# Attention scores turned in 64-row pieces: even rows into one PSUM bank, odd rows into the other

## The reference, cut to what matters

```python
a = softmax(q @ k.T * scale)      # 64 x 64 for each batch and head
o = a @ v
```

## Time and profile before

| what | us |
|---|---|
| median of 3 runs | 2369.84 (2367.78 to 2382.06) |
| the profiled execution | 2368.65 |
| its span, first to last instruction | 2366.8 |
| TensorE matmul busy | 2017.6 (85%) |
| VectorE busy | 1704.2 (72%) |
| ScalarE busy | 1203.9 (51%) |
| GpSimd busy | 1166.3 (49%) |

### The profile page before, as it was taken

One profiled execution on the slowest core, in us unless ns is written; L12 is line 12 of the kernel. 1 busy time (PEld: TensorE's weight loads), 2 busy tenths in 40 slices (PEclk: granted clock), 3 DMA queues, 4 the chain that ended last, 5 costly groups with the idle time before them and its releaser, 6 DMA issues.

```text
span 2366.8 us, 64773 instructions
## 1 busy us (share of the span) xinstructions
PE 2017.6 (85%) x25996; PEld 1681.2 (71%) x25996; DVE 1704.2 (72%) x4619; ACT 1203.9 (51%) x2802; POOL 1166.3 (49%) x1408
## 2 busy tenths in 40 slices
PE   5999989899899998998989685994888897997981
PEld 3976768777687776876767464993677786886981
DVE  6688787887878878888778984224888888874232
ACT  5356775466744677446755342552433342443540
POOL 3674346752367533675245543445554513214476
PEclk7999999999999999999999896997998998998996
DMA  3000000000000000000000018992001000117993
GB/s 139 4 7 1 2 1 4 5 3 2 2 4 5 3 2 1 4 5 3 2 37 2 20 40 216 347 351 79 22 17 28 14 8 16 35 37 240 351 336 94
DMA packets 98044, 147.33 MB, mean 62 GB/s; under 512 B 32016, under 2 KB 72464, under 8 KB 97488
## 3 DMA queue, kind: packets, MB, share of 16 engines
q1 hardware_dynamic: 88656, 124.55, 15.6%
q0 software_dynamic: 9088, 18.63, 3.0%
HBM read 126.55 MB, written 16.58 MB: 60 GB/s over the span
## 4 chain that ended last, share of the span: by engine, by line
PE 52%; DVE 25%; POOL 10%; issue 7%; ACT 4%; DMA 2%; SPq 0%; POOLq 0%; DVEq 0%; ACTq 0%
PE PS L636 5%; PE PS L2016 5%; PE PS L2000 5%; PE PS L1519 4%; PE PS L1525 4%; POOL GOT L1667 3%; PE PS L1023 3%; PE PS L988 2%; DVE mx L1017 2%; PE PS L1088 2%; DVE P L1019 2%; PE PS L1038 2%; DVE zo L612 2%; PE PS L1087 2%; PE PS L1119 2%
## 5 line engine op out<-in xcount | busy, mean ns | idle before, releaser
L2029 ACT ACTIVATE wh<-PS,we 128x128 f32<-128x128 f32 x624 | 176.4, 372 | 203.6 <-PE PS L2000 202.9
L1913 POOL DMA_INDIRECT wx<-x,INV x156 | 149.2, 956 | 179.5 <-PE PS L2007 136.1
L1017 DVE TENSOR_REDUCE mx<-PS 128x8 f32<-128x512 f32 x256 | 176.6, 690 | 36.7 <-PE PS L999 24.7
L616 POOL TENSOR_TENSOR xrs<-xrs,Cs 128x2 f32<-128x2 f32 x112 | 80.4, 717 | 234.4 <-DVE xrs L608 232.6
L2016 PE MATMUL PS<-we,wh 128*128 128x128 f32 x1248 | 172.1, 280 | 22.0 <-DVE wxT L2046 20.9
L2000 PE MATMUL PS<-wxT,we 128*128 128x128 f32 x1248 | 169.7, 283 | 22.1 <-issue 11.4
L1019 DVE TENSOR_TENSOR P<-PS,mx 128x512 f32<-128x512 f32 x256 | 176.9, 691 | 8.9
L1540 ACT ACTIVATE eh<-PS 128x256 f32<-128x256 f32 x256 | 96.8, 384 | 160.2 <-PE PS L1519 155.9
L2016 PEld LDWEIGHTS PS<-we,wh 128*128 128x128 f32 x1248 | 155.7, 193 | 28.4 <-DVE wxT L2046 26.7
L1023 PE MATMUL PS<-Cs,P 128*128 128x128 f32 x1024 | 157.0, 284 | 22.1 <-ACT P L1413 12.9
L2000 PEld LDWEIGHTS PS<-wxT,we 128*128 128x128 f32 x1248 | 157.0, 199 | 24.0 <-issue 12.2
(11 more groups left out here) (349 smaller groups left out, 5613.4 us busy)
## 6 DMA issues: line engine op xcount, KB each, us to landing
we<-in_wf SPq DMA_DIRECT2D x78, 578.0 KB, 6.1
we<-in_wl SPq DMA_DIRECT2D x78, 578.0 KB, 6.5
yf<-wy SPq DMA_DIRECT2D x78, 64.0 KB, 5.7
ys<-wy SPq DMA_DIRECT2D x78, 64.0 KB, 6.4
x<-X SPq DMA_DIRECT2D x32, 128.0 KB, 2.1
R<-in_wa SPq DMA_DIRECT2D x1, 3072.0 KB, 14.9
wx<-x,INV POOLq DMA_INDIRECT x156, 5.8
X<-in_x SPq DMA_DIRECT2D x4, 512.0 KB, 15.0
```

Of the source, the lines that this page charges most:

```text
L1017: e.tensor_reduce(A.mx[r], S3, AX, ALU.max).then_inc(*o.inc())
L1913: e.indirect_dma_start(out=WB[s].x[n_ % 2], out_offset=None, in_=x1[half_of(q)], in_offset=bass.IndirectOffsetOnAxis(ap=INV[half_of(q)][:, ...
L2029: i = e.activation(B.h[:, 128 * f:128 * f + 128], ps(s, 1)[:, 128 * f:128 * f + 128], ACT.Relu, bias=w[:, 512 + f:513 + f])
```

## The change

`pe_turn_p` now handles both r of a unit in one step. It takes the 128 x 128 transposes apart: for each r and k, the upper 64 partitions (parity 0) of `P[r]` go as a 64 x 128 block into bank 0, and the lower 64 (parity 1) as another into bank 1. A unit has 16 transposes of 64 moving columns in place of 8 of 128. The step waits for both exponentials (or masks) and raises one semaphore. ScalarE's two copies go bank by bank as before, but a bank now holds one parity of both r; they have one wait in front of them. `pe_heads` waits for both copies in either call, and finds its operand at another place of the same size. `STEPS` has one `a_pT` in the place of two, and the strings of `ORDER` for all engines and both lists are written anew (in the first sweep's list, TensorE has 64 steps less, and in the rest 64 less).

```diff
-        def pe_turn_p(e, dst, P):
-            for k in range(4):
-                i = e.transpose(dst[:, 128 * k:128 * k + 128], P[:, 128 * k:128 * k + 128], ID)
+        def pe_turn_p(e, s, P):
+            for r, k, p in product(range(2), range(4), range(2)):
+                a, c0 = slice(64 * p, 64 * p + 64), 64 * (4 * r + k)
+                i = e.transpose(ps(s, p)[:, c0:c0 + 64], P[r][a, 128 * k:128 * k + 128], ID[a, a])
             return i
...
             for q, i, p in product(range(2), range(2), range(2)):
-                c0, q0 = 66 * (2 * q + i), W * q + 128 * i + 64 * p
-                j = e.matmul(dst[64 * p:64 * p + 64, c0:c0 + 66], A.P[r][:, q0:q0 + 64],
+                c0, q0 = 66 * (2 * q + i), 256 * r + 64 * (2 * q + i)
+                j = e.matmul(dst[64 * p:64 * p + 64, c0:c0 + 66], A.P[p][:, q0:q0 + 64],
...
                 for r in range(2):
                     e.wait_ge(*(sig.at(G, "a_ex", a, u, r) if a else sig.at(G, "a_mk", u, r)))
-                    pe_turn_p(e, ps(s, r), A.P[r]).then_inc(*sig.inc(G, "a_pT", a, u, r))
-                    yield
+                pe_turn_p(e, s, A.P).then_inc(*sig.inc(G, "a_pT", a, u))
+                yield
                 for r in range(2):
-                    e.wait_ge(*sig.at(G, "a_pt", a, u, r))
+                    e.wait_ge(*sig.at(G, "a_pt", a, u, 1))
                     pe_heads(e, A, ps(s, r), r, u).then_inc(*sig.inc(G, "a_ops", a, u, r))
...
-                for r in range(2):
-                    e.wait_ge(*sig.at(G, "a_pT", a, u, r))
-                    e.activation(A.P[r], ps(s, r), ACT.Copy).then_inc(*sig.inc(G, "a_pt", a, u, r))
+                e.wait_ge(*sig.at(G, "a_pT", a, u))
+                for p in range(2):
+                    e.activation(A.P[p], ps(s, p), ACT.Copy).then_inc(*sig.inc(G, "a_pt", a, u, p))
                     yield
```

More of the change, by code:

```diff
@@ L70 @@
             "d_xps.2 d_pps.3 d_xps.3 d_ups.0 d_rps d_ups.1 d_ops d_oTp.0 d_oTp.1 d_so d_wo m_zT.0.0 a_vps.0.0 a_vps.0.1 a_qk.0.0 a_qk.0.1 a_s.0.0 "
[4 rows of a table removed]
[3 rows of a table added]
+            "turn.t",
         "act":
@@ L132 @@
         "pe":
-            "turn.n a_qk.n a_vps.n a_s.n.0 a_pT.n.0.0 a_pT.n.0.1 a_s.n.1 a_pT.n.1.0 a_pT.n.1.1 a_ops.n a_oTp.n n_lo.n turn.h h_up.0.0 h_up.0.1 h_up.1.0 "
-            "h_up.1.1 h_dn.0 h_up.2.0 h_up.2.1 h_dn.1 h_up.3.0 h_up.3.1 h_dn.2 h_up.4.0 h_up.4.1 h_dn.3 h_up.5.0 h_up.5.1 h_dn.4 h_up.6.0 h_up.6.1 h_dn.5 "
-            "h_up.7.0 h_up.7.1 h_dn.6 h_dn.7 turn.g q_lgp.g",
+            "turn.n a_qk.n a_vps.n a_s.n.0 a_pT.n.0 a_s.n.1 a_pT.n.1 a_ops.n a_oTp.n n_lo.n turn.h h_up.0.0 h_up.0.1 h_up.1.0 h_up.1.1 h_dn.0 h_up.2.0 "
+            "h_up.2.1 h_dn.1 h_up.3.0 h_up.3.1 h_dn.2 h_up.4.0 h_up.4.1 h_dn.3 h_up.5.0 h_up.5.1 h_dn.4 h_up.6.0 h_up.6.1 h_dn.5 h_up.7.0 h_up.7.1 h_dn.6 "
+            "h_dn.7 turn.g q_lgp.g",
         "act":
@@ new lines @@
+            "033032332123103113200123003203201221112313013330012022022121120130130200133122312101203003333201313010010013023301323221013110301030321020302002330001"
+            "233110321002222313323031031231113233223211123001002112023223012223103032002233300011211230330011030130101120222101121210120120003221333212231231221032"
+            "023001330131112332032002003303032132321223013010100323233032021211003011312331302020022303312331201310030012022301231323013201202032303211331021021021"
+            "3203210331113121223212332330213113121322321323132121323323231123",
@@ new lines @@
+            "123211112233033332222011000000001100000011111132323333332222121231111211222220032233000000003333011000001111113223222133333312222211111100222200330000"
+            "223333330000010001133113132333321112222221101120000322223333",
+        "act":
+            "400332211301211211233221133112001201212331012222330032333001121103200022110113132323112220033003332201013300022001113312222010111233321223101112004430"
+            "333221112201033002233322003330103101120002313220111122330202120033133322000003310012233001122330044013021320130213201302123001213230120132301201323012"
+            "013230120132301201323012223331110001111100110110110100112323023000021211223001133312222330333002220330110212211222112212121211322332331211332322311313"
+            "333033232132101120210201011100110333000212112211331312122132213313221331333212122133200011222000233321311223031120120202333202030030322233333300111212"
+            "203033100101022112233302011200222033002233010301131133310033222223000231334341311111100110110202020220211120200202223330033311310330022200110311330221"
+            "201011103332020121200303230102022211122000133311003011222322310102330301123301202200013233200332323032002220300330030300330300330000211123300112431320"
+            "123230121032032013320101302103210132321001323120013213200132120301321023",
@@ L245 @@
+            "7263704152601453726370415263107546745675498ab9addddb89abdddd89ddddab822dddd330011372615263726153704260415372604370426371504372615041504372615041537262"
+            "63157040415372637152604041537261326c50470415c37261526043c70415c372615023c764c47565c647ccccccccc",
     },
@@ L1036, in pe_heads8 @@
             for g, i, k, p in product(range(4), range(2), range(2), range(2)):
-                c0, q0 = 144 * i + 18 * (2 * g + k), W * i + 128 * k + 64 * p
-                j = e.matmul(dst[64 * p:64 * p + 64, c0:c0 + 18], A.P[2 * (g % 2) + g // 2][:, q0:q0 + 64],
+                c0, q0 = 144 * i + 18 * (2 * g + k), 256 * (g // 2) + 64 * (2 * i + k)
+                j = e.matmul(dst[64 * p:64 * p + 64, c0:c0 + 18], A.P[2 * (g % 2) + p][:, q0:q0 + 64],
                              A.V[:, 8 * (2 * i + p) + 2 * g + k, :, :].rearrange("p h d -> p (h d)"), True, True)
@@ L1388, in pe_small @@
                     e.wait_ge(*sig.at(G, "a_ex", y, h, r))
[L1389 to L1390 removed]
+                pe_turn_p(e, s, A.P[2 * h:2 * h + 2]).then_inc(*sig.inc(G, "a_pT", y, h))
+                yield
             for r in range(2):
@@ L1414, in act_small @@
                     yield
-                for r in range(2):
-                    e.wait_ge(*sig.at(G, "a_pT", y, h, r))
-                    e.activation(A.P[2 * h + r], ps(s, r), ACT.Copy).then_inc(*sig.inc(G, "a_pt", y, h, r))
+                e.wait_ge(*sig.at(G, "a_pT", y, h))
+                for p in range(2):
+                    e.activation(A.P[2 * h + p], ps(s, p), ACT.Copy).then_inc(*sig.inc(G, "a_pt", y, h, p))
                     yield
```

129 lines of the change are left out of this document (56 added, 73 removed), and 7 rows, old and new, of the table STEPS.

## The result

The changed kernel takes 2389.97 us (median of 16 runs, 2381.94 to 2408.76), the kernel before 2379.38 on the same chip (16 runs, 2366.05 to 2390.2): ratio 1.0059, 95% interval 1.0038 to 1.0080. By the ratio it is 14 us slower (10.6 by the medians); 2350 was forecast. Of the three runs of before that were known ahead of the prediction two lie near the low end of its 16 (2367.78 and 2369.84), as the profiled one does (2368.65). So 9.5 us of the 40 us between forecast and measurement come from the base that was taken (2369.84 for 2379.38), and some 30 from the change.

A forecast was written before the change was run, and what follows sets the result against it. The prediction took TensorE to bound the sweep, with VectorE not far behind, and both to bound the first narrow attention. TensorE's -25.4 us plus 6 us of waits gave -19.4, from 2368.65 to 2350 us; 8-in-10 range 2331 to 2388.

The forecast's parts named there:

- the term of the waits: Blocks waiting for both exponentials and copies, on TensorE's and ScalarE's queues: costs 6 us, between 0 and 39.
- half of 128 x 0.09: How the 6 us for waits was sized over 128 units, after TensorE's present waits before these transposes.
- At nothing: Copies, products' operands, new places and merged semaphore cost nothing; VectorE and GpSimd do the same work in another order.
- The stream: TensorE's transposes: 0.058 us a pair, 59.4 us in place of 111.6, so -52.2 us in all.
- The prediction's sign: In the changed profile's timeline, 16 transposes take 0.2 + 8 x 0.058, given as about 0.75 us.
- The rival of loads one after the other: Row halves cannot load together on TensorE, a pair costs 0.112 us: +18 us, 2387; chance 0.14.
- The changes of shape: On TensorE, 26, 17 and 57 more shape changes by stretch at 0.15 us each: 3.9, 2.6 and 8.6 us.
- TensorE's sum: Sweep -22.2, first narrow attention -10.5, second -4.5 us; by the shares of the path together -25.4 us.
- its share of the path: Part of the edited line's TensorE time that lies on the path: 0.70, 0.67 and 0.64 by stretch, 0.68 overall.
- The rival of the neighbours: VectorE, as full in later stretches, cancels savings there; later block starts cost 12 us in the sweep: 2366; chance 0.22.
- the three: The rivals: loads in a row 2387 (0.14), neighbours take it back 2366 (0.22), all of it arrives 2332 (0.07).

The follow-up runs named there:

- orders_only: Kernel before with the changed kernel's ORDER strings and both transposing calls in one step, old 128 x 128 transposes, waits and semaphores: 2403.1 us, ratio 1.0101.
- orders_and_waits: Changed kernel with its transposes put back to 128 x 128, keeping new strings and joined waits: 2410.69 us, ratio 1.0124 to the kernel before.
- halves_in_turn: Changed kernel with all 8 upper-row transposes of a unit before the 8 lower ones: 2437.63 us, ratio 1.0222 to the kernel before.
- change_behind_sweep: Kernel before with the changed kernel's transposes, joined waits and orders only in the narrow attentions behind the sweep: 2383.58 us, ratio 1.0032.
- orders_behind_sweep: Kernel before with the changed kernel's orders and merged steps only behind the sweep, old transposes: 2384.19 us, ratio 1.0016.

## Why the prediction was wrong

*The step that failed* is the term of the waits. It took 6 us between 0 and 39 "near the low end", because "the orders are rewritten, and the other slots' work fills the time". The merged step with its new strings costs 24 us (orders_only) and the joined waits 5.5 more, together 29.5 (24 to 35 by the interval): five times the term, inside its own ends. The 0.09 in its "half of 128 x 0.09" stands in no row. The argument from TensorE's present waits (21.5 us before these transposes) looked at the wrong place. It asked how long the block waits for its inputs, which the new strings keep short (TensorE's 26.2 us ahead of line 1026 in the changed kernel are little more), and not what the strings give up to keep it short: they had 80 pairs of calls with other slots' steps between them, and after the merge those slots come to line 626 too early: in the changed kernel, too, TensorE waits there 30.1 us in 75:1219 for 19.7.

*The clock* was in no term. The prediction noted that it was full nearly everywhere in the sweep and reckoned as if it stayed. It fell from 0.9349 to 0.9248, an estimated 17 to 21 us. Most of it comes with the new orders, 0.0084 in orders_only; there it can't be told apart from the waits, and 14 to 18 of the 24 us go with it. Behind the sweep it comes with the new shape. This is also why TensorE's busy time did not fall by the 50 us that were forecast (2017.2 for 2017.6), though the transposes' group fell by 60.

*"At nothing"* was said of VectorE and GpSimd doing the same work in another order. The runs with strings of their own show that an order is no free thing: 5 to 11%.

*The stream* was right in kind and 0.085 us short in size: 0.55 us for a block, not 0.464, 11 us over 128. The second pair starts 0.05 late, and the rest are 0.062 apart and not the 0.058 that were predicted: 0.05 and 8 x 0.004 make up nearly all of it. (The prediction's sign, 0.2 + 8 x 0.058, is 0.66 and not the 0.75 that it gives; the timeline has 0.71.) The rival of loads one after the other falls (0.58 us for sixteen loads, of which one takes 0.147 in the mean). The Trainium skill ("TensorEngine Tiling (Array Packing)", Key Properties) has it that tiles in different places load and multiply in parallel, and the trace agrees for two halves of the rows.

*The changes of shape* were right in number and nearly in price. The trace of the changed kernel has 1054 stretches of one shape where 1055 were counted from the strings; the step behind a block, 0.153 us from the last pair to line 1090 in the median, holds 0.094 of change (the further 0.10 for an fp32 load, which the prediction lists, is not seen there), and "issue" ahead of the loads is 15.1 us for 9.3. That the merged step alone leaves 911 was not in the count, so that the shape by itself adds 143 changes, 21 us, against the 100 of the whole change.

*TensorE's sum and its share of the path.* Per block 0.93 became 0.55: 49 us; less the 21 us for shapes 28 us. The traces agree: from the start of the matmul before a block to that of the one behind it, the changed kernel takes 0.217 us less than orders_and_waits in the mean of 83 blocks at full clock and without a long wait in either, 28 us over 128. Its gain in the whole was 15.7 (plus or minus 7): a share of 0.56, from 0.3 to 0.8, which holds the 0.68 that was taken. The 40 us put on by halves_in_turn came back as 39 (plus or minus 9), and as 22 to 25 without the clock's estimated part, a share near 0.6. So the share read off the chain before was fair both ways, as far as these runs tell.

*Sum as measured:* -15.7 + 24 + 5.5 = +14 us, as the 1.0059 says; predicted -25.4 + 6.

*The rival of the neighbours* named the right kind of mechanism, at 12 us, and only for VectorE. None of the three priced a loss of more than that from the strings.

What stays open: whether better strings for the merged step exist, and by how much of the 24 us; why the granted clock is lower with the new orders and, behind the sweep, with the new shape; and how much of the loss would stay if it were not. A step for each r in the new shape was not tried: its copy would read a bank while TensorE writes the other half of it.

## What to carry to other kernels

Where the order of many slots' steps is written out by hand, a change that merges two steps, or lets one wait for two, is priced first by what stood between them, and not by the lengths of the waits at the edited line. Run the change once with its steps and waits but without its gain (the kernel with new strings and old shapes): here it showed +1.2% that the gain of 0.66% could not repay. And read stage ends of one profile with the spread of a stage that was not touched, here 17 us between three executions of the same sweep. Set the granted clocks of the runs beside their times before a difference of 1% is put down to waits: here they go, by the estimate, with the whole of it.

## What was not expected of the hardware

- The two 64-row transposes of a pair start 3 or 4 ns apart, and the pairs 62 ns apart, but the second pair comes 111 ns behind the first (medians of 103 blocks): a block of this kind pays 0.05 us on top of the change of shape.
- The same sixteen transposes with all of one row half first take 0.31 us more: the order of the calls alone decides whether halves work side by side.
- From the sweep's end to the first mixture the granted clock is 0.79 to 0.81 with the new shape (of 1.0, that is 2.4 GHz, with stretches at 1.2), where the kernel before has 0.89 and the kernels that have the new orders with the old shape 0.85 and 0.86. For orders_only and change_behind_sweep:

```profile
1234.00:1460.00 226.00, 173.91 (x2414) 136.37 (x2412) 192.06 (x544) 98.20 (x196) 119.45 (x124) 0.86 0.14 45
```

```profile
1216.00:1447.00 231.00, 174.12 (x2672) 133.82 (x2673) 192.74 (x551) 97.72 (x196) 120.41 (x124) 0.81 0.14 44
```

In the middle of this stretch TensorE is idle more than half of 20 us in both kernels (busy 9.57 us from 1340 before, 7.05 us in the changed one, at 0.63 and 0.59). In the next 20 us the kernel before is at 1.00 with TensorE busy 16.97 us; the changed one is at 0.58 with 18.56. These are single executions, but the means of 12 runs, 0.9275 in change_behind_sweep and 0.9336 in orders_behind_sweep, go the same way. It fits that the shape gained nothing behind the sweep, but no run sets the clock apart from the shape.
